# Graph attention layer with experts: preparation in two passes over the node tiles, and eight groups of rows gathered before the graph stage

## The reference, cut to what matters

```python
# x: 6250 x 256 nodes; 100000 edges (src, dst) sorted by dst; edge_weight per edge
def _L0_gnn_ref(x, edge_index, edge_attr, W_l, b_l, W_r, b_r, att, bias):   # x is the layer-normed input
    x_l = (x @ W_l + b_l).reshape(n, H, C)        # H = 8 heads, C = 32
    x_r = (x @ W_r + b_r).reshape(n, H, C)
    x_j = x_l[src]
    g = jax.nn.leaky_relu(x_r[dst] + x_j, NEG_SLOPE)
    alpha = jnp.einsum('ehc,hc->eh', g, att) + jnp.log(edge_attr)[:, None]
    alpha = softmax over the edges of one dst      # segment max, exp, segment sum, + 1e-16
    out = jax.ops.segment_sum(x_j * alpha[..., None], dst, num_segments=n)
    return out.reshape(n, H * C) + bias
x = x + _L0_gnn_ref(_layernorm(x), ...)
x = x + _L0_ffn_ref(_layernorm(x))   # 8 experts, the two best per token, gelu between two products
```

## Time and profile before

| what | value |
| --- | --- |
| device time, median of 3 runs | 1835.51 us |
| lowest and highest | 1831.84 and 1836.99 us |
| span of the profiled execution | 1834.0 us |
| preparation | 0 to about 151 us |
| graph stage | 151 to about 1320 us |
| routing, experts | to 1834 us |
| busy over the span | PE 93%, DVE 77%, ACT 68%, POOL 71% |

### The profile page before, as it was taken

The page is one execution under the profiler, slowest core; times in us unless marked ns, Lnnn a source line. Parts: engine busy times, 40 slices in busy tenths (PEclk is TensorE's granted clock), DMA queues, the critical chain, the costliest instruction groups (busy, mean ns, idle before and its releaser), DMA issues. The chain is left out here.

```text
span 1834.0 us, 36250 instructions
## 1 busy us (share of the span) xinstructions
PE 1704.0 (93%) x9433; PEld 1449.1 (79%) x9434; DVE 1417.0 (77%) x2670; ACT 1250.3 (68%) x3163; POOL 1299.3 (71%) x1358
## 2 busy tenths in 40 slices
PE   6895789999999999999999999998797899999998
PEld 4674578887787888788888888876596799999998
DVE  6774689999999999999999999999868433333333
ACT  3463589999898999999999999987770133233222
POOL 4866777777777777777777777776435677776775
PEclk9997899999999999999999999999857999999999
DMA  6887777877877888777878888774674344444444
GB/s 224 225 267 248 220 235 239 240 242 238 238 243 236 240 241 240 238 244 243 235 245 239 241 241 243 240 236 130 202 244 166 73 78 70 72 71 69 70 73 52
DMA packets 214752, 359.18 MB, mean 196 GB/s; under 512 B 44062, under 2 KB 103880, under 8 KB 214457
## 3 DMA queue, kind: packets, MB, share of 16 engines
q1 hardware_dynamic: 150392, 208.33, 34.9%
q0 software_dynamic: 63072, 147.92, 33.3%
q10 hardware_dynamic: 1120, 1.05, 0.2%
HBM read 302.77 MB, written 54.40 MB: 195 GB/s over the span
## 5 line engine op out<-in xcount | busy, mean ns | idle before, releaser
L829 POOL DMA_INDIRECT rows<-left_rows,idx x880 | 841.1, 956 | 269.3 <-issue 263.9
L1191 PE MATMUL p_row<-rights,hotT 128*128 128x256 f32 x1760 | 504.0, 368 | 55.4 <-issue 26.0
L1193 PE MATMUL p_row<-rows,ident 128*128 128x256 f32 x1760 | 529.8, 383 | 0.0
L1254 PE MATMUL p_gain<-W,hots 128*128 128x264 f32 x1760 | 470.4, 391 | 8.7 <-DVE acc L1029 6.3
L1191 PEld LDWEIGHTS p_row<-rights,hotT 128*128 128x128 f32 x1760 | 322.0, 192 | 131.1 <-issue 82.1
L1254 PEld LDWEIGHTS p_gain<-W,hots 128*128 128x128 f32 x1760 | 324.0, 190 | 78.9 <-issue 24.6
L1081 ACT ACTIVATE L<-p_row 128x512 f32<-128x512 f32 x440 | 259.2, 589 | 127.0 <-PE p_row L1193 125.3
L1708 ACT ACTIVATE e_hT<-e_ph,b_column 128x128 f32<-128x128 f32 x420 | 119.7, 368 | 326.0 <-PE e_ph L1733 326.0
L1000 DVE TENSOR_TENSOR W<-rows,p_weights 128x1024 f32<-128x1024 f32 x220 | 266.9, 1213 | 43.9 <-PE p_gain L1254 41.4
L1151 ACT ACTIVATE far<-iota_row,dl 128x128 f32<-128x128 f32 x880 | 299.2, 391 | 0.0
L909 DVE TENSOR_TENSOR L<-L,p_weights 128x1024 f32<-128x1024 f32 x220 | 266.1, 1210 | 27.0 <-ACT L L1081 27.0
(11 more groups left out here) (254 smaller groups left out, 1880.7 us busy)
## 6 DMA issues: line engine op xcount, KB each, us to landing
rights<-right_rows SPq DMA_DIRECT2D x440, 256.0 KB
locals<-item_locals SPq DMA_DIRECT2D x110, 256.0 KB, 3.7
rows<-left_rows,idx POOLq DMA_INDIRECT x880
right_rows<-p_parts SPq DMA_DIRECT2D x49, 256.0 KB
w<-in_L_ffn_W SPq DMA_DIRECT2D x16, 512.0 KB, 6.4
left_rows<-p_y SPq DMA_DIRECT2D x49, 132.0 KB
kept_rows<-X SPq DMA_DIRECT2D x7, 896.0 KB, 4.4
X<-kept_rows SPq DMA_DIRECT2D x7, 896.0 KB, 4.9
```

The lines of the kernel that those rows point to most:

```text
L829: nc.gpsimd.indirect_dma_start(out=rows[:, g.slot(RINGS), n, :], out_offset=None, in_=d["left"][:, :], in_offset=bass.IndirectOffsetOnAxis ...
L1191: nc.tensor.matmul(to, hotT[:, g.slot(2), i, :], rights[:, g.slot(2), n, part * D:(part + 1) * D], start=(part == 0), stop=False)
L1193: last = nc.tensor.matmul(to, s["ident"][:, :], rows[:, g.slot(RINGS), i, 0:D], start=False, stop=True)
L1254: last = nc.tensor.matmul(p_gain[:, n, 0:D + H], hots[:, g.slot(2), i, :], W[:, g.slot(2), i, :, :].rearrange("p h c -> p (h c)"), start=( ...
```

## The change

- The node tiles are gone through twice. The first loop normalises, turns and makes the left rows of all 49 tiles; the turned tile is kept in `X`, over the rows that it came from. The second loop makes the right rows from `X`.
- PSUM `p_py` is four slots of one side instead of two of both sides. Left and right stores have semaphores of their own.
- The output bias is put into the left rows (b_l + bias), the right bias becomes b_r - bias. The left bias had not been in the left rows before. Nodes without edges get bias * 1e-16 into the sums, by GpSimd.
- The bias rows are added for half the tiles (even left ones, odd right ones) by TensorE, with a product of a row of ones with the bias row, and for the others by VectorE (`copy_left`, `take_right`). ScalarE copies the even left tiles, VectorE the odd ones. High and low part of the odd right tiles are taken from PSUM. All low parts are VectorE's.
- `kept_rows` is gone: after the graph stage the rows are loaded from x itself.
- GpSimd does no residual adds. It gathers src, dst and weights in this order, and, when the left rows are stored and as the right half leaves parts of `X`, the first eight groups of left rows. `idx` and its copies are gone, the gathers read `srcs`.
- x comes in four pieces instead of three, and the item steps stand at other tiles.

```diff
+EARLY_GROUPS = 8
-PIECES = ((0, BY), (BY, 4 * BY), (4 * BY, 7 * BY))
+PIECES = ((0, BY), (BY, 2 * BY), (2 * BY, 4 * BY), (4 * BY, 7 * BY))
...
+                pool.wait_ge(turned_copied, QI)
+                for k in range(4):
+                    pool.wait_ge(left_stored[k], 16 * len(range(k, NODE_TILES, 4)))
+                for g in range(EARLY_GROUPS):
+                    pool.wait_ge(right_projected, min(NODE_TILES, -(-(g + 1) * G * DL // D)))
+                    wait(pool, gathered[g % RING], g // RING * (16 * G))
+                    for n in range(G):
+                        gather_item(nc, d, s, g, n)
...
+                def multiply(t, slot, side, wide, biased, done):
+                    for h in range(KD):
+                        last = nc.tensor.matmul(py[:, slot, 0:wide], X[:, t, h * P:(h + 1) * P],
+                                                W[:, h, side, 0:wide], start=(h == 0), stop=(h == KD - 1 and not biased))
+                    if biased:
+                        pe.wait_ge(biases_done, 2)
+                        last = nc.tensor.matmul(py[:, slot, 0:D], s["ones"][0:1, :], side_bias[0:1, side, :], start=False, stop=True)
+                    last.then_inc(done, 1)
...
+                def project_right(t):
+                    if t < 4:
+                        pe.wait_ge(*left_of(NODE_TILES + t - 4))
+                    else:
+                        pe.wait_ge(low_done, t - 3)
+                    multiply(t, right_slot(t), 1, D, t % 2 == 1, right_projected)
...
+                def copy_left(t):
+                    v.wait_ge(left_projected, t + 1)
+                    wait(v, left_stored[t % 4], 16 * (t // 4))
+                    v.wait_ge(biases_done, 2)
+                    nc.vector.tensor_copy(y[:, t % 4, D:DL], py[:, t % 4, D:DL])
+                    nc.vector.tensor_tensor(y[:, t % 4, 0:D], py[:, t % 4, 0:D], side_bias[:, 0, :], ALU.add).then_inc(left_by_vector, 1)
...
                 def take_high(t):
-                    v.wait_ge(right_steps, 2 * t + 1)
-                    nc.vector.tensor_scalar(parts[:, t % 4, 0, :].bitcast(I32), right[:, t % 4, :].bitcast(I32),
+                    wait(v, right_stored[t % 4], 16 * (t // 4))
+                    if t % 2:
+                        v.wait_ge(right_projected, t + 1)
+                    else:
+                        v.wait_ge(right_steps, t // 2 * 3 + 1)
+                    nc.vector.tensor_scalar(parts[:, t % 4, 0, :].bitcast(I32), right_of(t).bitcast(I32),
                                             LOW_BITS, LOW_BITS, ALU.logical_shift_right, ALU.logical_shift_left).then_inc(right_steps, 1)
...
                 def gather(g):
...
+                    if g.n >= EARLY_GROUPS:
+                        wait(pool, weighed, g.n - (RINGS - 1))
+                        wait(pool, gathered[g.slot(RING)], g.turn(RING) * (16 * G))
+                        for n in range(G):
+                            gather_item(nc, d, s, g.n, n)
```

More of the change, by code:

```diff
@@ L167, in build @@
             pass
+        s["gathered"] = [nc.alloc_semaphore(f"g_gathered{i}") for i in range(RING)]
         s["rows"] = keep("rows", [P, RINGS, G, DL])
@@ L268, in blocks_in, with left_of, right_slot @@
             return min(P, EB - c * P)
[L270 to L274, removed]
+        def left_of(t):
+            return (left_by_vector, (t + 1) // 2) if t % 2 else (left_by_scalar, t // 2 + 1)
+        def right_slot(t):
+            return (NODE_TILES + t) % 4
         with nc.Block(no_gpsimd_drain=True) as block:
@@ L319, in _ @@
[L319 to L338, removed]
@@ new lines, in _ @@
+                pool.wait_ge(biases_in, 48)
+                nc.gpsimd.memset(no_edges[:, :, C:C + 1], 0.0)
+                nc.gpsimd.tensor_scalar(no_edges[:, :, 0:C], bias_rows[:, 2, :].rearrange("p (h c) -> p h c", c=C), 1e-16, None, ALU.mult)
+                pool.wait_ge(items_done, 1)
+                for rows, table, landed in ((rows_s, "src", src_in), (rows_d, "dst", dst_in), (rows_w, "weight", weight_in)):
+                    for q in range(QI):
+                        nc.gpsimd.indirect_dma_start(
+                            out=rows[:, q, :], out_offset=None, in_=d[table][:, :],
+                            in_offset=bass.IndirectOffsetOnAxis(ap=t_idx[:, q:q + 1], axis=0),
+                        ).then_inc(landed, 16)
@@ L534, in _ @@
+                act.wait_ge(floored, 1)
+                nc.scalar.activation(rows_w[:, :, :], rows_w[:, :, :], ACT.Ln).then_inc(logged, 1)
+                for q in range(QI):
+                    copy_back(2 * QI + q, s["logw"])
             @block.vector
@@ L693, in _, with gather_item @@
                         last.then_inc(breaks_done, 1)
+def gather_item(nc, d, s, g, n):
+    i = g * G + n
+    nc.gpsimd.indirect_dma_start(
+        out=s["rows"][:, g % RINGS, n, :], out_offset=None, in_=d["left"][:, :],
+        in_offset=bass.IndirectOffsetOnAxis(ap=s["srcs"][:, i:i + 1], axis=0),
+    ).then_inc(s["gathered"][g % RING], 16)
 def node_tiles(eng, regs, s, g):
@@ L732, in edges @@
     matched, cleared = sem("g_matched"), sem("g_cleared")
-    listed = sem("g_listed")
-    gathered = [sem(f"g_gathered{i}") for i in range(RING)]
+    gathered = s["gathered"]
     rights_in = [sem(f"g_rights_in{i}") for i in range(2)]
@@ L887, in _ @@
                 v.wait_ge(cleared, 2)
-                def list_sources(g):
-                    if g.c % TURN == 0:
-                        for r in range(RING):
-                            wait(v, gathered[r], (g.turn(RING) - 2) * (16 * G))
-                        nc.vector.tensor_copy(idx[:, parity(g), :], s["srcs"][:, bass.ds(g.n * G, CHUNK)]).then_inc(listed, 1)
-                def list_ahead(g):
-                    if not isinstance(g.n, int) or g.n > 0:
-                        list_sources(g)
                 def empty(g):
```

344 lines of the change are left out of this document (168 added, 176 removed).

## The result

| | before | changed |
| --- | --- | --- |
| device time, median of 13 runs | 1836.99 us | 1842.9 us |
| lowest and highest | 1831.84 and 1841.7 | 1836.35 and 1847.79 us |
| ratio (95% interval) | 1 | 1.0026 (1.0014 to 1.0037) |
| span of the profiled execution (its own time) | 1834.0 us | 1834.4 us (1836.35) |
| graph stage starts at | 151.1 us | 181.9 us |

The change costs 0.3% where a gain of 0.9% was forecast, and the time lies outside the range. The graph stage did about what was forecast. The preparation is 30.8 us longer instead of 9, and that outweighs it.

A forecast was written before the change was run, and what follows sets the result against it. The graph stage was taken to be paced by GpSimd's 880 gathers. Graph stage -25 us and preparation +9 us gave -16 us on the span of 1834.0: span 1818, time 1819.5 us, range 1804 to 1837.

The forecast's parts named there:

- The preparation in halves: Preparation: left half ends at 95 us, right at 156, graph stage starts about 160 instead of 151.1; +9 us (-3 to +20).
- The store rings: Right half of the preparation: waits for four store buffers of 256 KB add 4 us, making 61 us.
- VectorE's 57 us of the sum: Right half of the preparation: VectorE's mean 0.97 us a tile plus 9 us of item work once, 57 us.
- The early gathers: Right half of the preparation: eight groups, 52 us even at 6.5 each, just hidden in about 60 us; nothing charged.
- The graph stage: Graph stage: eight groups gathered ahead take 40 us off GpSimd's path, about 25 kept; -25 us (17 to 30).
- ring waits: Graph stage, ring of 16: GpSimd waits 10 to 18 us in all for weighings around groups 16 to 22.
- the 0.5 us named as a sign of being wrong: Graph stage: eight groups still take about 40 us; forecast wrong if that period changes by over 0.5 us.
- the first product: Start of the graph stage: comes 4 to 5 us behind it, without a wait for gathered rows.
- group 11: Graph stage's fill: reaches VectorE about 52 us behind the stage's start instead of 73.3; 21.6 us won (17 to 27).
- the 42 us of the sum: Graph stage's fill: eleven steps, five of 4.07 us and six of 3.6, 42 us (bounds 36 and 46).
- Rival 3: Right half bound by stores landing in four buffers: 1.7 us a tile, 84 us, stage at 183, 1843 us; chance 0.09.
- Rivals 1, 2 and 4: 1: preparation no longer, 1810 us, 0.20; 2: head start given back, 1835, 0.14; 4: VectorE locks GpSimd out, 1840, 0.03.

The follow-up runs named there:

- e2: Changed kernel with the bias product over 128 rows of ones and bias/128 instead of one row each; ratio to the kernel before 0.9975.
- e5: Changed kernel with 128-row bias products and seven buffers instead of four for left rows and right-row parts; 1821.07 us, ratio to the kernel before 0.9913.
- e3: Changed kernel with no group gathered ahead of the graph stage (EARLY_GROUPS = 0); ratio to the kernel before 1.0129.
- e1: Changed kernel with all bias rows added by VectorE, none by TensorE; ratio to the kernel before 0.9963.
- e4: Changed kernel with the weights turned back at right tiles 24 to 30 instead of 10 to 16; ratio to the kernel before 1.0039.
- e6: Changed kernel with 128-row bias products on odd right tiles, and left bias rows added by VectorE; ratio to the kernel before 0.9944.
- e8: Changed kernel with bias products of 32 rows on left tiles and 64 on right ones; product 0.62 to 0.63 us, graph stage starts at 183.7 us.
- all four edits: Changed kernel, left bias by VectorE, right by 128-row products, rings of seven, twelve groups ahead, node tiles' store at tile 40; 1815.0 us, ratio to before 0.9878.

## Why the prediction was wrong

- **The step that failed** is in "The preparation in halves": "I take 0.44, since the columns are the same". A bias product of one row costs 0.77 us in the left and 0.82 in the right half, 0.63 of it its own. The bounds given, 0.22 to 0.44, did not hold the value: the nearest rows were all of full products, and the reason for the upper end (equal columns) was an assumption. It cost 18 us of TensorE's time and 12.2 us of the stage's start (e2 against changed).
- **The store rings** are the second term mis-sized: 4 us in the right half and nothing in the left one (the 5 us there were for item steps and small transfers). Rings of seven give back 9.7 us alone (3.5 left, 6.2 right) and 10.9 beside e2 (1.5 left, 9 right, the rest behind the last product). With them and the 128-row product the right half takes 56.1 us, as VectorE's 57 us of the sum. The store of the node tiles, a small transfer by its bytes, was the one that filled the queues in the left half. In the kernel before it did so too (issued at 56.8 us; 52 GB/s at a share of 1.08 from 60 to 64 us), and TensorE rested 2.6 of the 8 us behind that.
- **The early gathers were charged at nothing.** They cost 5.0 us of the right half with rings of four (e3). They were hidden behind TensorE, as forecast (GpSimd was done 19.9 us early), but not beside the stores, for which VectorE waited 4.1 us more with them. The cover was named for the wrong resource.
- These overlap, so they don't sum to more than the 21.9 us by which the stage is later than forecast: with the first two undone (e5) it starts at 158.8.
- **The graph stage** was right: last gather 26.4 us earlier (forecast 25), ring waits 16.3 us (10 to 18), eight groups of VectorE in 39.1 us from group 24 to 32 (157.7 - 118.6 behind the stage's start). Against the 39.75 of before that one pair is over the 0.5 us named as a sign of being wrong; from group 24 to 208 the mean is 40.0 us against 40.15, which is not. Of the fill's steps the first product was 2.5 us late, for the rights, and group 11 therefore 3.5 us. Steps took 42.7 / 11 = 3.9 us on the mean, as the 42 us of the sum had it.
- **Rival 3**, slower at 1843 us with the stage at 183, hit both numbers by another way. Its mechanism, a right tile of 1.7 us bound by landing, isn't there: the right half is 69 us, not 84, and 24 x 0.82 = 20 us of these are bias products. Rivals 1, 2 and 4 fell: the preparation got 30.8 us longer, the ring took back about 14 of GpSimd's 40 us, as forecast, and not 31, and a group gathered ahead took about 5 us.
- **One reading needs care.** The profiled execution of the changed kernel was its fastest run. Its last weighing lies at 1131 us behind the stage's start; in e1, e2, e4, e5 and with rings alone it lies at 1138 to 1141 (e6: 1136), with the last gather within 3 us of the same place. So the usual gain of the graph stage is 20 to 23 us, not 30, and by it a usual run loses 8 to 11 us, against 5.9 by the medians. Most of the difference arises in VectorE's last steps, from group 216 (1080.5 us against 1082.8 in e1) to 219 (1098.5 against 1107.4); its cause is open, no run tried it. Group 11 too is early in this trace, at 55.2 us; in e1, e2, e4 and e5 it comes at 57.3 to 58.5, so the fill usually wins 15 or 16 us where 21.6 were forecast.

## What to carry to other kernels

Before adding a product with fewer rows to a loop of full ones, measure it there: one with 128 rows and a scaled operand gives the same sum and was a third cheaper here (0.43 against 0.63 us). When a loop's period gets much shorter, its store rings must be recounted in periods, and a transfer must be judged by its packets, not by its bytes alone. Work that is moved under cover needs cover on each resource that it uses: here an idle engine, but not an idle store ring.

## What the runs showed of the hardware that was not expected

- An fp32 product of 256 columns between full ones, at a granted clock of 1.00, holds TensorE for 0.62 to 0.63 us with 1, 32 or 64 rows, and for 0.43 us with 128 (changed, e8, e2). The weight load of the shorter product and the next full one each start behind 0.33 to 0.34 us of idle time.
- A store of 896 packets of 4 bytes (3.5 KB) held the queues at a busy share of 0.82 to 1.20 for 8 us, with 41 to 54 GB/s moved (e2); without it the same stretch moved 124 to 213 GB/s (all four edits).
